# Token normalisation by bn_stats and ScalarE, and a projection moved behind the transposes, in a MetaFormer layer

## The chip, the cores and the metric

The kernel runs on one core of a Trainium2 chip. The metric is the device time of one execution in microseconds; before the change it is 7429.9 us, the median of 3 runs (7426.01 to 7444.18).

The names used here: TensorE (PE in the profile; PEld is its loading of weights) multiplies matrices, VectorE (DVE), ScalarE (ACT) and GpSimd (POOL) work on elements, SyncE (SP) issues transfers. SBUF is the memory beside the engines, PSUM the one that TensorE writes to. All of them run on their own and meet at semaphores.

## The reference, cut to what matters

```python
x = x + conv_ref(ln_c(x), wq, wk, wv, wo, rq, rk, rv, Gq, Gk, Gv1, Gv2)   # x: (4, 256, 128, 128) f32
t = to_tokens(x)                               # rows of 128 along w; 32768 tokens an image
t = t + ffn_ref(ln_t(t), gate_w, gate_b, weight1, weight2)

def ln_t(v, eps=1e-5):
    m = mean(v, axis=-1); s = var(v, axis=-1)
    return (v - m) / sqrt(s + eps)

# in ffn_ref: logits = x @ gate_w.T + gate_b (64 experts), softmax over the tokens,
# the 8 best tokens of each expert, the experts' two layers on them, added back to these tokens
```

Here conv_ref is an attention within each image row with relative terms, and ends in a 1x1 projection `wo`. The change lies between that projection and the logits: the sum with `x`, the normalisation ln_t of each row of 128, and the gate's logits. The reference is in float32 and so is all of the kernel.

## The kernel before, in words

The kernel is five phases that run one after the other: weights are prepared, q, k and v are projected, the attention is computed, `combine` finishes the attention and computes the gate's logits, and `experts` does the rest. The change touches `combine` alone.

`combine` works on 64 chunks, 16 for each of 4 images. A chunk is 8 image rows of all 256 channels: on the 128 partitions lie the channels of one half, so a chunk is two halves of 128 x 1024, or 16 groups (tokens) of 128 elements on each partition. Buffers come in pairs, used by even and odd chunks (`u`). For a chunk k the steps are:

- SyncE loads the two parts of the attention's sum (`sum_v`, `sum_r`) and x, 1 MB each in two transfers. The load of x waits for the residual of chunk k-2.
- GpSimd adds the two parts into `att` (line 888), after all six transfers have landed.
- TensorE projects (`project_out`, line 906): four blocks of 128 x 512, one for each PSUM bank of `y_ps`. Each block is two float32 matmuls, which the profile lists as four passes, so 16 passes a chunk. A block waits until VectorE has read the same bank of the chunk before.
- VectorE adds x to each block (`residual`, line 947); the result is `x1`.
- VectorE and ScalarE normalise with the class `LayerNorm`: VectorE sums each row (line 196), scales the 16 sums to means (line 198), subtracts them (line 203); ScalarE squares (line 207); VectorE sums the squares (line 212) and makes the variance (line 214); ScalarE takes the root (line 218); VectorE inverts it and refines the inverse in four short operations (lines 224 to 230) and multiplies (line 232) into `tn`.
- ScalarE issues the two stores of `x1` to the output (line 998), between the root and its next work.
- TensorE turns `tn` in 16 transposes (line 921) in four groups of four; ScalarE copies each group out of PSUM into `tnt` (line 1004). There are two banks for the turned groups, so a group waits for the copy of the group two before it.
- TensorE multiplies `tnt` by the gate (line 927) into `l_ps`, and ScalarE adds the bias and keeps the logits (`keep`, line 989).

The order on each engine is written out by hand, in a function `body(k, u, place)`, where `place` is 0 for an image's first chunk, 1 for the second, 14 and 15 for the last two, and 2 for the rest:

- TensorE's body: the projection of chunk k+2 (but at places 14 and 15), then the wait for `tn` of chunk k, its transposes, its logits. At place 0 it first projects k and k+1.
- VectorE's body: sums, means and centring of chunk k; the residual of chunk k+1; variance; inverse; the wait for the transposes that last read the buffer; the multiplication.
- ScalarE's body: the square of chunk k, `keep` of chunk k-1, the root of k, the stores of k, the four copies of k.

At the end of an image VectorE searches the logits for each expert's 8 largest, and ScalarE takes their exponentials, before the next image's chunks.

Of the kernel before, what the change touches and what calls it, by code (L numbers as in the profile page):

```python
# [17 lines left out]
P = 128  # L18
ALU = mybir.AluOpType
# [152 lines left out]
ROWS = 8  # L172
# [632 lines left out]
def combine(nc, d):  # L805

    with ExitStack() as ctx:
# [19 lines left out]
        y_ps = s.ps("y_ps", [P, 4, BANK])  # L828
        t_ps = s.ps("t_ps", [P, 2, BANK])
        l_ps = s.ps("l_ps", [P, 2, BANK])  # L830
        ln = LayerNorm(s, TOKEN_EPS)
        consts_loaded, ident_zero, ident_ready, gate_turned, gate_ready = (s.sem(n) for n in ("consts_loaded", "ident_zero", "ident_ready", "gate_turned", "gate_ready"))
        loaded = [s.sem(f"loaded{u}") for u in range(2)]
        att_ready, y_done, x1_ready, centred, tn_ready = (s.sem(n) for n in ("att_ready", "y_done", "x1_ready", "centred", "tn_ready"))
        turned, tnt_ready, l_done, l_ready = (s.sem(n) for n in ("turned", "tnt_ready", "l_done", "l_ready"))
        x1_stored = [s.sem(f"x1_stored{u}") for u in range(2)]
        cleared, topped, found, negated, summed, cand_stored = (s.sem(n) for n in ("cleared", "topped", "found", "negated", "summed", "cand_stored"))
# [55 lines left out]
        def _(pe):  # L893
# [3 lines left out]
            pe.transpose(t_ps[:, 0, 0:EXPERTS], gate[:, :], ident[0:EXPERTS, 0:EXPERTS]).then_inc(gate_turned, 1)  # L897
            pe.wait_ge(gate_ready, 1)

            def project_out(k, u):  # L900
                pe.wait_ge(att_ready, 2 * k + 6)
                for b in range(4):
                    sub, o = b // 2, b % 2
                    pe.wait_ge(x1_ready, 4 * k + b + 5)
                    for a in range(CHALF):
                        last = pe.matmul(y_ps[:, b], wo[:, a, o * P:(o + 1) * P], att[u][:, a, sub * BANK:(sub + 1) * BANK],  # L906
                                         start=a == 0, stop=a == CHALF - 1)
                    last.then_inc(y_done, 1)

            def body(k, u, place):  # L910
                if place == 0:
                    project_out(k, 0)
                    project_out(k + 1, 1)
                if place < PER - 2:
                    project_out(k + 2, u)
                pe.wait_ge(tn_ready, k + 1)
                for q in range(4):
                    pe.wait_ge(tnt_ready, 4 * k + q + 1)
                    a, rows = q // 2, range(4 * (q % 2), 4 * (q % 2) + 4)
                    for r, i in enumerate(rows):  # L920
                        last = pe.transpose(t_ps[:, q % 2, r * P:(r + 1) * P], tn[u][:, a * ROWS + i, :], ident[:, :])
                    last.then_inc(turned, 1)
                pe.wait_ge(tnt_ready, 4 * k + 6)
                for sub in range(2):
                    pe.wait_ge(l_ready, 2 * k + sub + 1)
                    for a in range(CHALF):
                        last = pe.matmul(l_ps[a * EXPERTS:(a + 1) * EXPERTS, sub], gate_t[:, :], tnt[:, 2 * a + sub, :], start=True, stop=True,
                                         tile_position=(0, a * EXPERTS))
                    last.then_inc(l_done, 1)
# [3 lines left out]
        @block.vector  # L933
        def _(dve):
            dve.sem_inc(x1_ready, 8)
            dve.wait_ge(gate_turned, 1)
            dve.tensor_copy(gate_t[:, :], t_ps[:, 0, 0:EXPERTS]).then_inc(gate_ready, 1)

            def residual(k, u, half_k):
                for b in range(4):  # L940
                    sub, o = b // 2, b % 2
                    dve.wait_ge(y_done, 4 * k + b + 9)
                    if b == 0:
                        dve.wait_ge(loaded[u], 8 * DMAS * k - 8 * DMAS * u + 16 * DMAS)
                        dve.wait_ge(x1_stored[u], 16 * k - 16 * u + 32)
                    at = slice(sub * BANK, (sub + 1) * BANK)
                    dve.tensor_tensor(x1[u][:, o, at], y_ps[:, b], x[u][:, o, at], ALU.add).then_inc(x1_ready, 1)  # L947

            def body(k, u, place):
                if place == 0:  # L950
                    residual(k, 0, 0)
                dve.wait_ge(x1_ready, 4 * k + 12)
                rows = x1[u][:, :, :].rearrange("c a (i w) -> c (a i) w", w=W)
                ln.mean_of(dve, rows, k)
                ln.centre(dve, rows, k).then_inc(centred, 1)
                if place < PER - 1:
                    residual(k + 1, 1 - u, 0)
                ln.variance(dve, k)
                dve.wait_ge(turned, 4 * k + 4)
                ln.scale(dve, tn[u][:, :, :], k).then_inc(tn_ready, 1)  # L960

            def best(n):
                dve.wait_ge(l_ready, 2 * PER * n + 2 * PER + 2)
# [12 lines left out]
        def _(act):  # L976
            act.sem_inc(turned, 8)
            act.sem_inc(tnt_ready, 2)
            act.sem_inc(l_ready, 2)
            act.sem_inc(cand_stored, 48)  # L980
            for u in range(2):
# [8 lines left out]
                                   ACT.Identity, bias=gate_b[:, :]).then_inc(l_ready, 1)  # L990

            def body(k, u, place):
                ln.square(act, centred, k + 1)
                if place:
                    keep(k - 1)
                ln.root(act, k)
                for a in range(CHALF):
                    act.dma_start(x1_out[bass.ds(k // PER, 1), :, a, bass.ds((k % PER) * CHUNK, CHUNK)].rearrange("n c x -> (n c) x"),
                                  x1[u][:, a, :]).then_inc(x1_stored[u], 16)
                for q in range(4):  # L1000
                    act.wait_ge(turned, 4 * k + q + 9)
                    if q == 0:
# [353 lines left out]
```

## Time and profile before

| | |
|---|---|
| median of 3 runs | 7429.9 us (7426.01 to 7444.18) |
| profiled execution, its own time | 7456.45 us |
| span of the profiled execution | 7454.4 us |
| granted TensorE clock, mean | 0.906 |
| busy: TensorE, its weight loads | 6396.6 us (86%), 5001.9 us (67%) |
| busy: VectorE, ScalarE, GpSimd | 5357.6 us (72%), 4765.6 us (64%), 2480.9 us (33%) |
| `combine`, by its first and last instructions | about 5854 to 7035 us of the span |

How to read it: a page and the answers of a query show one execution. Times are microseconds unless marked ns. A line such as `L232 DVE TENSOR_TENSOR comb_tn<-comb_ln_xc,...` names the source line, the engine, the operation and the tiles written and read. "x64" is a count.
### The profile page before, as it was taken

The numbers are of one execution on the slowest core, as the hardware profiler recorded it, in microseconds if no ns is written. First come the engines' busy times: TensorE is split into PE (matmuls) and PEld (weight loads), VectorE is DVE, ScalarE is ACT, GpSimd is POOL, SyncE is SP. The second block draws the span as 40 slices with busy tenths as digits, with TensorE's granted clock in tenths as the row PEclk, the third lists the DMA queues.
The fourth block names the chain that finished last, engine by engine and source line by source line (L and its number), as shares of the span: only waits on it lengthen the run. The fifth ranks groups of instructions, "written<-read, shape, count | busy, mean of one in ns | idle before, by whom it ended". The sixth has DMA issues, their size and how long they took to land. (4 is left out here: it accounts for less than half of the span.)

```text
span 7454.4 us, 279833 instructions
## 1 busy us (share of the span) xinstructions
PE 6396.6 (86%) x106442; PEld 5001.9 (67%) x106442; DVE 5357.6 (72%) x20905; ACT 4765.6 (64%) x11171; POOL 2480.9 (33%) x1267
## 2 busy tenths in 40 slices
PE   4999999969999989999998999989999767576558
PEld 3555555568888878888887888878888423232258
DVE  5444444448888878888887888878788788898820
ACT  0444444448988888888898898889889334343300
POOL 0000000025455545545554454544454323232110
PEclk6999999969999999999999999999999888898855
DMA  8555555557777677767677777777776767586422
GB/s 218 203 203 203 203 203 203 193 90 124 126 132 125 120 128 133 126 118 136 122 127 132 119 127 133 127 123 125 125 129 115 218 214 242 188 268 195 143 97 96
DMA packets 1197408, 1146.42 MB, mean 154 GB/s; under 512 B 625632, under 2 KB 956000, under 8 KB 1194144
## 3 DMA queue, kind: packets, MB, share of 16 engines
q1 hardware_dynamic: 1006816, 842.59, 54.6%
q10 hardware_dynamic: 188352, 285.27, 10.5%
q8 instruction: 795, 13.03, 0.9%
q14 instruction: 421, 3.45, 0.2%
q0 software_dynamic: 1024, 2.09, 0.1%
HBM read 708.04 MB, written 421.56 MB: 152 GB/s over the span
## 5 line engine op out<-in xcount | busy, mean ns | idle before, releaser
L788 POOL TENSOR_TENSOR att_scores<-att_scores,att_inverse 128x1024 f32<-128x1024 f32 x1024 | 1994.1, 1950 | 2047.0 <-DVE att_inverse L736 2046.8
L697 ACT ACTIVATE att_scores<-att_scores,att_negmax 128x128 f32<-128x128 f32 x8192 | 2572.9, 394 | 27.9 <-issue 13.2
L751 DVE CUSTOM_DVE_ANT_0 att_scores<-att_ps,att_scores 128x128 f32<-128x128 f32 x8192 | 1818.2, 289 | 773.1 <-PE att_ps L614 748.4
L603 PE MATMUL att_ps<-att_qk,att_rs 32*128 32x64 f32 x32768 | 2189.2, 280 | 107.1 <-issue 56.9
L603 PEld LDWEIGHTS att_ps<-att_qk,att_rs 32*128 32x128 f32 x32768 | 2034.2, 196 | 117.0 <-issue 110.0
L614 PE MATMUL att_ps<-att_own 32*128 32x128 f32 x16384 | 1822.0, 323 | 226.7 <-DMA att_own<-qk 150.0
L614 PEld LDWEIGHTS att_ps<-att_own 32*128 32x128 f32 x16384 | 1601.9, 198 | 512.5 <-issue 493.1
L656 PE MATMUL att_ps<-att_scores,att_rv 128*16 128x64 f32 x32768 | 1402.3, 330 | 39.0 <-issue 33.0
L690 ACT ACTIVATE att_scores<-att_ps 128x1024 f32<-128x1024 f32 x1024 | 1041.3, 1017 | 558.3 <-PE att_ps L603 528.7
L734 DVE TENSOR_REDUCE att_total<-att_scores 128x8 f32<-128x1024 f32 x1024 | 1242.2, 1213 | 0.0
L656 PEld LDWEIGHTS att_ps<-att_scores,att_rv 128*16 128x16 f32 x32768 | 1134.5, 119 | 71.6 <-issue 61.7
L369 PE MATMUL proj_qk_ps<-proj_xn,proj_w_qk 128*128 128x512 f32 x2048 | 902.8, 594 | 33.1 <-DVE proj_xn L232 33.1
L337 ACT ACTIVATE proj_qk_out<-proj_qk_ps 128x512 f32<-128x512 f32 x512 | 323.7, 632 | 613.5 <-PE proj_qk_ps L369 605.5
L369 PEld LDWEIGHTS proj_qk_ps<-proj_xn,proj_w_qk 128*128 128x128 f32 x2048 | 390.1, 191 | 470.5 <-issue 463.9
L906 PE MATMUL comb_y_ps<-comb_att,comb_wo 128*128 128x512 f32 x1024 | 514.3, 660 | 219.4 <-DVE comb_x L947 193.6
L751 DVE DVE_READ_ACCUMULATOR2_ANT att_negmax<- 128x1 f32 x8192 | 691.5, 84 | 0.3
L644 PE MATMUL att_ps<-att_scores,att_vt 128*16 128x128 f32 x16384 | 674.9, 282 | 17.0 <-issue 9.1
L784 POOL TENSOR_TENSOR att_rs<-att_rs,att_gain 128x1024 f32<-128x1024 f32 x64 | 122.4, 1913 | 1650.7 <-DMA att_rs<-in_L_conv_rk_dram 1650.7
L888 POOL TENSOR_TENSOR comb_att<-comb_sum_v,comb_sum_r 128x1024 f32<-128x1024 f32 x128 | 328.7, 2587 | 822.3 <-DMA comb_x<-in_x_dram 704.2
L906 PEld LDWEIGHTS comb_y_ps<-comb_att,comb_wo 128*128 128x128 f32 x1024 | 211.3, 212 | 527.3 <-issue 274.7
L377 PE MATMUL proj_v_ps<-proj_w_v,proj_xn 128*128 128x256 f32 x2048 | 462.9, 379 | 0.0
L377 PEld LDWEIGHTS proj_v_ps<-proj_w_v,proj_xn 128*128 128x128 f32 x2048 | 389.1, 190 | 107.5 <-issue 61.2
(147 smaller groups left out, 4986.3 us busy)
## 6 DMA issues: line engine op xcount, KB each, us to landing
qk<-proj_qk_out ACTq DMA_DIRECT2D x64, 2048.0 KB, 8.6
att_qk<-qk SPq DMA_DIRECT2D x512, 256.0 KB, 6.0
att_own<-qk SPq DMA_DIRECT2D x1024, 128.0 KB, 4.5
proj_x<-in_x_dram SPq DMA_DIRECT2D x128, 512.0 KB, 4.4
v_t<-proj_v_out ACTq DMA_DIRECT2D x64, 1024.0 KB, 11.7
att_vt<-v_t SPq DMA_DIRECT2D x256, 256.0 KB, 5.3
att_v<-att_att_v SPq DMA_DIRECT2D x1024, 64.0 KB, 3.8
att_r<-att_att_r SPq DMA_DIRECT2D x1024, 64.0 KB, 2.7
```

Of the source, the lines that this page charges most:

```text
L369: last = pe.matmul(qk_ps[:, j], w_qk[:, a, 4 * j:4 * j + 4].rearrange("c h t e -> c (h t e)"), xn[u][:, a, sub * BANK:(sub + 1) * BANK], s ...
L377: last = pe.matmul(v_ps[:, b, r * C:(r + 1) * C], xn[u][:, a, row * W:(row + 1) * W], w_v[:, a, :], start=a == 0, stop=a == CHALF - 1)
L603: return pe.matmul(ps[:, 4 + gg, jj * IU:(jj + 1) * IU], rs[32 * g:32 * g + 32, j, :], qk[v % 2][32 * g:32 * g + 32, :, j, :], start=True, ...
L614: return pe.matmul(ps[:, g, r * W:(r + 1) * W], own[half][32 * g:32 * g + 32, 1, at // PAIR, :, at % PAIR], own[half][32 * g:32 * g + 32, ...
L644: last = pe.matmul(ps[32 * g:32 * g + HD, 6, r * W:(r + 1) * W], vt[i // HROWS][:, i % HROWS, :], scores[v % BUFS][:, i, :], start=True, s ...
L656: last = pe.matmul(ps[32 * g:32 * g + HD, 7, jj * IU:(jj + 1) * IU], rv[:, j, :], scores[v % BUFS][:, :, j], start=True, stop=True, tile_p ...
L690: act.activation(scores[o % BUFS][:, :, :].rearrange("w i (g j) -> w i g j", g=G)[:, :, pair:pair + 2, t // 2 * JB:(t // 2 + 1) * JB], ps[ ...
L697: last = act.activation(scores[v % BUFS][:, i, :], scores[v % BUFS][:, i, :], ACT.Exp, bias=negmax[v % BUFS][:, i:i + 1], scale=-1.0)
L734: dve.tensor_reduce(piece(total[v], k), piece(scores[v], k), AX_X, ALU.add).then_inc(summed, 1)
L751: last = dve.tensor_tensor_reduce(out=scores[v][:, i, :], in0=ps[:, 2 * (p % 2) + r // HR, (r % HR) * W:(r % HR + 1) * W], in1=scores[v][: ...
L788: pool.tensor_tensor(piece(scores[v], p), piece(scores[v], p), piece(inverse[v], p).unsqueeze(3).broadcast_to([P, 2, HR, W]), ALU.mult).th ...
L906: last = pe.matmul(y_ps[:, b], wo[:, a, o * P:(o + 1) * P], att[u][:, a, sub * BANK:(sub + 1) * BANK], start=a == 0, stop=a == CHALF - 1)
```

## The change

The normalisation in `combine` no longer uses the class `LayerNorm`. VectorE takes mean and variance of two rows at a time with `bn_stats`, eight times for a chunk; the two rows are interleaved by the access pattern, as even and odd elements, so that one instruction gives both rows' count, mean and sum of squared deviations. One short operation makes the variance plus epsilon. After ScalarE's root, VectorE inverts and refines as before, and one more short operation makes `shift`, minus the mean times the inverse. ScalarE then normalises straight from `x1`: 16 activations of 128 x 128, each with its group's inverse as scale and its shift as bias.

The order changes with it. ScalarE's body is `keep` of k-1, root of k, stores of k, the 16 normalisations of k, the four copies of k. VectorE's body is the statistics of k, the residual of k+1, and inverse and shift of k; the residual now also waits until ScalarE has normalised the chunk that held the `x1` buffer before. TensorE's body is the wait for the normalised chunk, the first two groups of transposes, blocks 0 and 1 of the projection of k+2, the last two groups, blocks 2 and 3 of that projection, and the logits.

```diff
--- before.py
+++ after.py
@@ -828,10 +828,13 @@
         y_ps = s.ps("y_ps", [P, 4, BANK])
         t_ps = s.ps("t_ps", [P, 2, BANK])
         l_ps = s.ps("l_ps", [P, 2, BANK])
-        ln = LayerNorm(s, TOKEN_EPS)
+        stats = s.sb("stats", [P, GROUPS // 2, 2, 3])
+        var, std, inv, square, shift = (s.sb(n, [P, GROUPS]) for n in ("var", "std", "inv", "square", "shift"))
         consts_loaded, ident_zero, ident_ready, gate_turned, gate_ready = (s.sem(n) for n in ("consts_loaded", "ident_zero", "ident_ready", "gate_turned", "gate_ready"))
         loaded = [s.sem(f"loaded{u}") for u in range(2)]
-        att_ready, y_done, x1_ready, centred, tn_ready = (s.sem(n) for n in ("att_ready", "y_done", "x1_ready", "centred", "tn_ready"))
+        att_ready, y_done, x1_ready, tn_ready = (s.sem(n) for n in ("att_ready", "y_done", "x1_ready", "tn_ready"))
+        measured, var_ready, rooted, inverted, squared, corrected, refined, shifted = (
+            s.sem(n) for n in ("measured", "var_ready", "rooted", "inverted", "squared", "corrected", "refined", "shifted"))
         turned, tnt_ready, l_done, l_ready = (s.sem(n) for n in ("turned", "tnt_ready", "l_done", "l_ready"))
         x1_stored = [s.sem(f"x1_stored{u}") for u in range(2)]
         cleared, topped, found, negated, summed, cand_stored = (s.sem(n) for n in ("cleared", "topped", "found", "negated", "summed", "cand_stored"))
@@ -897,9 +900,10 @@
             pe.transpose(t_ps[:, 0, 0:EXPERTS], gate[:, :], ident[0:EXPERTS, 0:EXPERTS]).then_inc(gate_turned, 1)
             pe.wait_ge(gate_ready, 1)
 
-            def project_out(k, u):
-                pe.wait_ge(att_ready, 2 * k + 6)
-                for b in range(4):
+            def project_out(k, u, blocks=range(4)):
+                if 0 in blocks:
+                    pe.wait_ge(att_ready, 2 * k + 6)
+                for b in blocks:
                     sub, o = b // 2, b % 2
                     pe.wait_ge(x1_ready, 4 * k + b + 5)
                     for a in range(CHALF):
@@ -911,15 +915,15 @@
                 if place == 0:
                     project_out(k, 0)
                     project_out(k + 1, 1)
-                if place < PER - 2:
-                    project_out(k + 2, u)
-                pe.wait_ge(tn_ready, k + 1)
+                pe.wait_ge(tn_ready, k + 3)
                 for q in range(4):
                     pe.wait_ge(tnt_ready, 4 * k + q + 1)
                     a, rows = q // 2, range(4 * (q % 2), 4 * (q % 2) + 4)
                     for r, i in enumerate(rows):
                         last = pe.transpose(t_ps[:, q % 2, r * P:(r + 1) * P], tn[u][:, a * ROWS + i, :], ident[:, :])
                     last.then_inc(turned, 1)
+                    if q % 2 and place < PER - 2:
+                        project_out(k + 2, u, (q - 1, q))
                 pe.wait_ge(tnt_ready, 4 * k + 6)
                 for sub in range(2):
                     pe.wait_ge(l_ready, 2 * k + sub + 1)
@@ -933,6 +937,7 @@
         @block.vector
         def _(dve):
             dve.sem_inc(x1_ready, 8)
+            dve.sem_inc(shifted, 1)
             dve.wait_ge(gate_turned, 1)
             dve.tensor_copy(gate_t[:, :], t_ps[:, 0, 0:EXPERTS]).then_inc(gate_ready, 1)
 
@@ -943,21 +948,35 @@
                     if b == 0:
                         dve.wait_ge(loaded[u], 8 * DMAS * k - 8 * DMAS * u + 16 * DMAS)
                         dve.wait_ge(x1_stored[u], 16 * k - 16 * u + 32)
+                        dve.wait_ge(tn_ready, k + 1)
                     at = slice(sub * BANK, (sub + 1) * BANK)
                     dve.tensor_tensor(x1[u][:, o, at], y_ps[:, b], x[u][:, o, at], ALU.add).then_inc(x1_ready, 1)
 
             def body(k, u, place):
                 if place == 0:
                     residual(k, 0, 0)
+                dve.wait_ge(shifted, k + 1)
                 dve.wait_ge(x1_ready, 4 * k + 12)
-                rows = x1[u][:, :, :].rearrange("c a (i w) -> c (a i) w", w=W)
-                ln.mean_of(dve, rows, k)
-                ln.centre(dve, rows, k).then_inc(centred, 1)
+                rows = x1[u][:, :, :].rearrange("c a (b r w) -> c (a b) w r", r=2, w=W)
+                for g in range(GROUPS // 2):
+                    last = dve.bn_stats(stats[:, g].rearrange("c r m -> c (r m)"), rows[:, g])
+                last.then_inc(measured, 1)
+                dve.wait_ge(measured, k + 1)
+                dve.tensor_scalar(var[:, :].rearrange("c (g r) -> c g r", r=2), stats[:, :, :, 2], 1.0 / W, TOKEN_EPS, ALU.mult, ALU.add).then_inc(var_ready, 1)
                 if place < PER - 1:
                     residual(k + 1, 1 - u, 0)
-                ln.variance(dve, k)
-                dve.wait_ge(turned, 4 * k + 4)
-                ln.scale(dve, tn[u][:, :, :], k).then_inc(tn_ready, 1)
+                dve.wait_ge(rooted, k + 1)
+                dve.wait_ge(tn_ready, k + 2)
+                dve.reciprocal(inv[:, :], std[:, :]).then_inc(inverted, 1)
+                dve.wait_ge(inverted, k + 1)
+                dve.tensor_tensor(square[:, :], inv[:, :], inv[:, :], ALU.mult).then_inc(squared, 1)
+                dve.wait_ge(squared, k + 1)
+                dve.scalar_tensor_tensor(out=square[:, :], in0=square[:, :], scalar=-0.5, in1=var[:, :], op0=ALU.mult, op1=ALU.mult).then_inc(corrected, 1)
+                dve.wait_ge(corrected, k + 1)
+                dve.scalar_tensor_tensor(out=inv[:, :], in0=square[:, :], scalar=1.5, in1=inv[:, :], op0=ALU.add, op1=ALU.mult).then_inc(refined, 1)
+                dve.wait_ge(refined, k + 1)
+                dve.scalar_tensor_tensor(out=shift[:, :].rearrange("c (g r) -> c g r", r=2), in0=stats[:, :, :, 1], scalar=-1.0,
+                                         in1=inv[:, :].rearrange("c (g r) -> c g r", r=2), op0=ALU.mult, op1=ALU.mult).then_inc(shifted, 1)
 
             def best(n):
                 dve.wait_ge(l_ready, 2 * PER * n + 2 * PER + 2)
@@ -976,6 +995,7 @@
         def _(act):
             act.sem_inc(turned, 8)
             act.sem_inc(tnt_ready, 2)
+            act.sem_inc(tn_ready, 2)
             act.sem_inc(l_ready, 2)
             act.sem_inc(cand_stored, 48)
             for u in range(2):
@@ -990,13 +1010,19 @@
                                    ACT.Identity, bias=gate_b[:, :]).then_inc(l_ready, 1)
 
             def body(k, u, place):
-                ln.square(act, centred, k + 1)
                 if place:
                     keep(k - 1)
-                ln.root(act, k)
+                act.wait_ge(var_ready, k + 1)
+                act.activation(std[:, :], var[:, :], ACT.Sqrt).then_inc(rooted, 1)
                 for a in range(CHALF):
                     act.dma_start(x1_out[bass.ds(k // PER, 1), :, a, bass.ds((k % PER) * CHUNK, CHUNK)].rearrange("n c x -> (n c) x"),
                                   x1[u][:, a, :]).then_inc(x1_stored[u], 16)
+                act.wait_ge(shifted, k + 2)
+                act.wait_ge(turned, 4 * k + 4)
+                for r in range(GROUPS):
+                    last = act.activation(tn[u][:, r, :], x1[u][:, r // ROWS, (r % ROWS) * W:(r % ROWS + 1) * W], ACT.Identity,
+                                          bias=shift[:, r:r + 1], scale=inv[:, r:r + 1])
+                last.then_inc(tn_ready, 1)
                 for q in range(4):
                     act.wait_ge(turned, 4 * k + q + 9)
                     if q == 0:
```

## Rows read from the trace of the kernel before

**Rows 1.** The page: span, and busy time of each engine with its share.

```profile
span 7454.4 us, 279833 instructions
...
PE 6396.6 (86%) x106442; PEld 5001.9 (67%) x106442; DVE 5357.6 (72%) x20905; ACT 4765.6 (64%) x11171; POOL 2480.9 (33%) x1267
```

**Rows 2.** Groups by line, 5840 to 7050 us: busy, mean ns | idle before.

```profile
...
L232 DVE TENSOR_TENSOR comb_tn<-comb_ln_xc,comb_ln_inv 128x2048 f32<-128x2048 f32 x64 | 146.7, 2292 | 2.2
...
L989 ACT ACTIVATE comb_logits<-comb_l_ps,comb_gate_b 128x512 f32 (+1 forms) x128 | 131.5, 1121 | 11.4 <-PE comb_l_ps L927 11.3
L198 DVE TENSOR_SCALAR comb_ln_mean<-comb_ln_t 128x16 f32<-128x16 f32 x64 | 127.0, 1985 | 2.2
```

**Rows 3.** Window: busy PE, PEld, DVE, ACT, POOL; PEclk; DMA share; GB/s.

```profile
...
5870.00:6100.00 230.00, 169.37 (x564) 77.19 (x562) 215.29 (x208) 90.80 (x115) 79.11 (x31) 0.93 0.81 269
```

**Rows 4.** Line 232 in each image: duration min/median/max in ns, first and last start.

```profile
L232 DVE TENSOR_TENSOR comb_tn<-comb_ln_xc,comb_ln_inv x16: 2291/2292/2293, 5876.5 to 6113.1; 128x2048 f32<-128x2048 f32 x16
...
L232 DVE TENSOR_TENSOR comb_tn<-comb_ln_xc,comb_ln_inv x16: 2291/2292/2294, 6183.1 to 6419.3; 128x2048 f32<-128x2048 f32 x16
...
L232 DVE TENSOR_TENSOR comb_tn<-comb_ln_xc,comb_ln_inv x16: 2291/2292/2293, 6490.2 to 6722.6; 128x2048 f32<-128x2048 f32 x16
...
L232 DVE TENSOR_TENSOR comb_tn<-comb_ln_xc,comb_ln_inv x16: 2291/2292/2293, 6793.2 to 7020.7; 128x2048 f32<-128x2048 f32 x16
```

**Rows 5.** Timeline of all engines, 5999.5 to 6012.7 us: start, duration, engine, line.

```profile
...
5999.92 0.82 SPq L875 DMA_DIRECT2D comb_x<-in_x_dram  x2
...
6002.32 0.22 ACT L218 ACTIVATE comb_ln_std<-comb_ln_var 128x16 f32<-128x16 f32 x1 [1.72 <-DVE comb_ln_var L214]
...
6002.63 0.85 ACTq L998 DMA_DIRECT2D out_dram<-comb_x  x2
...
6003.56 2.29 DVE L232 TENSOR_TENSOR comb_tn<-comb_ln_xc,comb_ln_inv 128x2048 f32<-128x2048 f32 x1
...
6004.99 5.39 POOL L888 TENSOR_TENSOR comb_att<-comb_sum_v,comb_sum_r 128x1024 f32<-128x1024 f32 x2 [10.62 <-DMA comb_x<-in_x_dram]
...
6005.98 1.09 PE L921 MATMUL comb_t_ps<-comb_ident,comb_tn 128*128 128x128 f32 x8 [0.70 <-DVE comb_tn L232]
6006.75 1.09 ACT L1004 ACTIVATE comb_tnt<-comb_t_ps 128x512 f32<-128x512 f32 x2 [4.21 <-PE comb_t_ps L921]
...
6008.08 2.33 DVE L198 TENSOR_SCALAR comb_ln_mean<-comb_ln_t 128x16 f32<-128x16 f32 x1
```

**Rows 6.** Timeline of TensorE alone, 5850 to 6420 us, idle before in brackets.

```profile
...
5875.37 9.96 PE L906 MATMUL comb_y_ps<-comb_att,comb_wo 128*128 128x512 f32 x16 [3.77 <-POOL comb_att L888]
...
6160.39 9.11 PE L906 MATMUL comb_y_ps<-comb_att,comb_wo 128*128 128x512 f32 x16 [29.61 <-DVE comb_x L947]
...
6185.55 3.85 PE L921 MATMUL comb_t_ps<-comb_ident,comb_tn 128*128 128x128 f32 x16 [6.50 <-DVE comb_tn L232]
6190.17 3.68 PE L927 MATMUL comb_l_ps<-comb_tnt,comb_gate_t 128*64 128x512 f32 x8 [0.76 <-ACT comb_tnt L1004]
...
6201.39 1.04 PE L921 MATMUL comb_t_ps<-comb_ident,comb_tn 128*128 128x128 f32 x8
6202.76 1.15 PE L921 MATMUL comb_t_ps<-comb_ident,comb_tn 128*128 128x128 f32 x8 [0.33 <-ACT comb_tnt L1004]
6204.67 1.94 PE L927 MATMUL comb_l_ps<-comb_tnt,comb_gate_t 128*64 128x512 f32 x8 [0.76 <-ACT comb_tnt L1004]
6207.32 7.13 PE L906 MATMUL comb_y_ps<-comb_att,comb_wo 128*128 128x512 f32 x16 [0.71 <-DVE comb_x L947]
...
6406.78 3.68 PE L921 MATMUL comb_t_ps<-comb_ident,comb_tn 128*128 128x128 f32 x16 [10.07 <-DVE comb_tn L232]
6411.22 1.94 PE L927 MATMUL comb_l_ps<-comb_tnt,comb_gate_t 128*64 128x512 f32 x8 [0.76 <-ACT comb_tnt L1004]
```

**Rows 7.** Line 697's exponentials on ScalarE: duration min/median/max in ns.

```profile
...
L697 ACT ACTIVATE att_scores<-att_scores,att_negmax x8192: 376/388/458, 1579.4 to 5807.1; 128x128 f32<-128x128 f32 x200
```

**Rows 8.** Timeline of ScalarE in the attention stage, 3002 to 3006 us.

```profile
...
3002.62 2.48 ACT L697 ACTIVATE att_scores<-att_scores,att_negmax 128x128 f32<-128x128 f32 x8
```

## The prediction, made before the changed kernel was run

> **What bounds the kernel now.** I read the page's first part, then the combine stage alone (the change touches nothing else): its groups by line, its busy time by window, and one chunk as a timeline. The profiled execution takes 7456.45 us, its span 7454.4 us [rows 1]. In 230 us of steady combine work VectorE is busy 215.3 us, TensorE 169.4 us, ScalarE 90.8 us, at a granted TensorE clock of 0.93 and a DMA share of 0.81 [rows 3]. VectorE is the bound: a chunk puts four passes over 2048 elements on it (the last, line 232, takes 2.29 us [rows 2]) and a negligible-looking scaling of 16 means that takes 1.99 us on average [rows 2], because it is held: in the timeline it starts at 6008.08 while GpSimd runs since 6004.99, and ends at 6010.41, when GpSimd ends at 6010.38 [rows 5]. The period of a chunk comes from line 232: per image 16 executions, first to last start 236.6, 236.2, 232.4 and 227.5 us [rows 4], together 932.7 us for 60 periods, 15.55 us each. TensorE's projection hides in it, issued ahead of the wait for the normalised chunk, while VectorE and ScalarE still work on that chunk.
>
> **The order after the change.** I followed the semaphores round one chunk before pricing anything. ScalarE's body for chunk k starts with keep(k-1), which waits for the logits of k-1. Only then, in order, come the root for k, the two stores' issue, the wait for the shifts, 16 normalisations, the signal that the chunk is ready. TensorE's body for k now starts with the wait for that signal; the projection stands behind it, and the logits of k stand behind both halves of the projection. And keep(k), with which ScalarE's next body starts, needs these logits. So the two engines take turns: TensorE's whole body, then ScalarE's keep, root and normalisations, then TensorE again. Nothing of one body overlaps the other but four copies out of PSUM. Before, the projection (7.13 us [rows 6]) ran beside VectorE's work; now it is in the ring. The period is the sum of the ring.
>
> **Term by term.**
> - VectorE loses its four long passes and the held scaling and gains 8 bn_stats, of 256 elements each. No row shows one; the 2.29 us for 2048 elements gives 0.29 us each in proportion, 2.3 us in all; the ends are 0.17 us each (below the 128x16 operations' own time nothing runs here) and 2.29 us each. They run for chunk k+1 while ScalarE normalises k and TensorE works on k: cover of more than 15 us, so I count nothing at either end but the very last (18 us), which would be late by a few us. VectorE stops being the bound; what is late next is the ring.
> - Hand-over from normalised chunk to TensorE: 0.13 us (line 232 ends at 5.85, the transpose starts at 5.98 [rows 5]).
> - TensorE at the full clock: 8 transposes 1.04, half a projection 3.56, 8 transposes 1.15, half a projection 3.56, logits 1.94 [rows 6]: 11.25 us. The copies between them (1.09 us for two [rows 5]) lie beside the first half and the second. I keep 11.2.
> - TensorE's clock: after the ring's ScalarE part TensorE has been idle for some 9 us. Rows show what an idle stretch does: after 3.77 and 29.6 us idle a projection of 16 passes takes 9.96 and 9.11 us instead of 7.13, mean 2.4 us more; after 6.5 us idle transposes and logits take 3.85 and 3.68 us, logits at half their pace, yet after 10.07 us idle the clock is back for the logits, 1.94 us [rows 6]. So each body starts at 1.2 GHz and recovers inside it. Ends: nothing (the clock stays up), and half pace throughout, 1.9 + 1.9 for transposes, 14.3 for the projection, 3.68 for the logits, 10.6 us more than 11.2. I take 2.9: the 2.4 of a projection plus half of the 0.9 that cold first transposes cost (3.85/2 against 1.04).
> - Logits to root: two keeps of 1.12 us [rows 2], the first begun when half of the logits is there: 1.15 us past the end of the logits.
> - Root to shifts: from the root's start (6002.32) to line 232's (6003.56) 1.24 us [rows 5], plus one more operation like those between, 0.2, and a hand-over: 1.48 us. The stores' issue (0.85 us on ScalarE's queue [rows 5]) lies beside it.
> - 16 normalisations of 128x128. The nearest row is the exponential of line 697: 388 ns each alone [rows 7], 8 back to back in 2.48 us [rows 8], 0.30 us from start to start. Ends: 15 x 0.30 + 0.39 = 4.9 us with full overlap, 16 x 0.458 (its longest [rows 7]) = 7.3 us. I take 16 x 0.388 = 6.2 us, without overlap, because each reads two operands per partition (bias and scale) where the exponential reads one.
>
> The Trainium skill (ScalarE: Activation LUTs, What ACT_TABLE_LOAD costs) says that an operand given per partition adds about 93 ns to an ACTIVATE and that neighbours overlap by about 93 ns. The 388 ns and the 0.30 us from start to start agree with it for one such operand; no row has two. By that page 16 would take about 6.3 us, an estimate; by the row's own overlap 4.9.
>
> Ring: 0.13 + 11.2 + 2.9 + 1.15 + 1.48 + 6.2 = 23.06 us, against 15.55. Memory does not bind it: 0.81 x 15.55 = 12.6 us of transfer a chunk [rows 3]. GpSimd's addition runs two chunks ahead.
>
> In an image 14 periods hold a projection; the 15th does not: transposes and logits with their gap, 6.4 to 8.3 us by the rows after idling [rows 6], say 7.4, and 0.13 + 1.15 + 1.48 + 6.2: 16.4 us. So 14 x 23.06 + 16.4 = 339.2 us an image, 1357 us for four, against 932.7: +424 us. The head of an image loses a square and a reduction and gains the 16 normalisations; I count nothing, within 1 us an image. The candidates' search is untouched. Profiled execution 7456.45 + 424 = 7880; it lies 26.5 us above the median of the runs (7429.9), so the forecast is 7854 us.
>
> **The rivals.**
> - The clock is not lost, because projection, transposes and logits now stand close together: the ring is 20.2 us, 56 x 2.9 = 162 us less, 7692 us; with the overlapped normalisations too 7619. For it: the one body after 10 us of idling that recovered in its transposes. Against: every body now follows a long idle stretch.
> - The clock never recovers: 10.6 instead of 2.9, 56 x 7.7 = 431 us more, 8285 us. For it: the transposes and logits that ran at half pace through all 8.3 us [rows 6]. Against: both projections after idling ended less than 3 us late.
> - GpSimd holds the short VectorE operations of root to shifts, as it holds the scaling of the means: 2.33 - 0.17 = 2.16 us a chunk, 60 x 2.16 = 130 us, 7984 us. It decides when GpSimd starts inside these 1.3 us. GpSimd starts 5.07 us after the load of x is issued (5999.92 to 6004.99 [rows 5]), and that load now follows the last residual, about 0.8 us after the projection; root to shifts runs 3.3 to 4.6 us after the projection. By that it is 1.3 us clear. The Trainium skill (SBUF — State Buffer, Who interferes with whom) calls this an exclusive lock and extends it to VectorE operations with two SBUF inputs, which three of these are; the held scaling agrees, and no row here shows it for two inputs.
> - Other side, faster: TensorE and ScalarE do overlap, and the relief of VectorE shows. The place is keep(k-1) at the head of ScalarE's body: if the part beside TensorE's 11.2 us fitted into 4.3 us the period would pass below 15.55. Keep, root and hand-over take 2.8 of these, so the 16 normalisations would have to take 1.5 us, under 0.1 us each, a third of the tightest spacing that a row shows. Then the transfers' 12.6 us would bound: 60 x 2.95 = 177 us less, 7253 us.
> - The change doesn't do what it says: VectorE's relief and the ring cancel. That takes a ring of 15.5 us, and the same 0.1 us each.
>
> **How the numbers follow.** Forecast 70%, own range 7700 to 8000 (normalisations 4.9 to 7.3 us, clock 1.7 to 4.2: 20.5 to 25.5 us of ring, 56 of each). Clock kept 10%, clock never back 7%, GpSimd in the way 8%, faster 3%, cancelled 2%. From 7690 to 8010 the forecast, most of the GpSimd case and part of the clock case are inside. A change of 0.3% (22 us) is what a measurement can tell; slower 95%, same 2%, faster 3%.
>
> **What would show it.** In the changed kernel TensorE idle for 8 to 10 us between logits and first transpose, its releaser the normalisations; ScalarE waiting for the logits before keep; the first transposes and part of the first half of the projection at 1.2 GHz, the second half at 2.4; normalisations from start to start near 0.39 us; VectorE under half busy, its small operations between root and shift 0.2 us each. Wrong it is if keep(k-1) starts before the second half of the projection has ended, or if the period stays under 18.8 us (the ring at the full clock with overlapped normalisations).

## The result, and the profile after

The changed kernel takes 7794.72 us (median of 4 runs, 7783.66 to 7805.79) against 7427.95 us before (median of 4 runs; the 7429.9 us of the first table are the median of three of them): 1.0492 times as long, 95% interval 1.0475 to 1.0509, 367 us more. The forecast was 7854 us, slower, with a range from 7690 to 8010. The profiled execution of the changed kernel lies 11 us above its median, the one before 28.5 us, so the two profiles differ by less than the medians: 7803.8 against 7454.4 us of span [rows 1], 349 us.

The page, and 220 us of the first image by window (columns as in [rows 3]):

```profile
span 7803.8 us, 280727 instructions
...
PE 6427.9 (82%) x106442; PEld 5044.1 (65%) x106442; DVE 4916.4 (63%) x21161; ACT 5042.9 (65%) x12131; POOL 2456.5 (31%) x1267
```

```profile
5890.00:6110.00 220.00, 128.58 (x400) 64.45 (x400) 75.44 (x181) 107.26 (x236) 48.74 (x22) 0.78 0.59 194
```

VectorE lost 441 us of work over the kernel and is busy for 34% of the stage instead of 94%. No engine is busy for more than 59% of it. The relief is real and the stage is longer: engines wait for each other. How long a chunk takes, by the shift (line 978), which every chunk makes once; first and last start of each image, as in [rows 4]:

```profile
L978 DVE SCALAR_TENSOR_TENSOR comb_shift<-comb_stats,comb_inv x16: 174/175/176, 5863.0 to 6184.3; 128x16 f32<-128x16 f32 x16
...
L978 DVE SCALAR_TENSOR_TENSOR comb_shift<-comb_stats,comb_inv x16: 174/174/176, 6257.6 to 6577.4; 128x16 f32<-128x16 f32 x16
...
L978 DVE SCALAR_TENSOR_TENSOR comb_shift<-comb_stats,comb_inv x16: 174/174/176, 6650.9 to 6972.1; 128x16 f32<-128x16 f32 x16
...
L978 DVE SCALAR_TENSOR_TENSOR comb_shift<-comb_stats,comb_inv x16: 174/175/176, 7045.1 to 7365.8; 128x16 f32<-128x16 f32 x16
```

Together 1283.0 us for 60 periods, 21.4 us each, against 932.7 us and 15.55 before: 350 us more, which is all of the difference between the two profiles. One period on the timeline of all engines:

```profile
6033.00 1.94 PE L931 MATMUL comb_l_ps<-comb_tnt,comb_gate_t 128*64 128x512 f32 x8
...
6034.27 2.00 ACT L1009 ACTIVATE comb_logits<-comb_l_ps,comb_gate_b 128x512 f32 x2 [3.95 <-PE comb_l_ps L931]
...
6036.07 0.22 ACT L1016 ACTIVATE comb_std<-comb_var 128x16 f32<-128x16 f32 x1
...
6037.24 0.18 DVE L978 SCALAR_TENSOR_TENSOR comb_shift<-comb_stats,comb_inv 128x16 f32<-128x16 f32 x1
6037.45 2.74 DVE L962 BATCH_NORM_STATS2 comb_stats<-comb_x 128x6 f32<-128x256 f32 x8
6037.54 6.26 ACT L1023 ACTIVATE comb_tn<-comb_x,comb_shift,comb_inv 128x128 f32<-128x128 f32 x16 [1.25 <-DVE comb_shift L978]
...
6040.26 4.65 POOL L891 TENSOR_TENSOR comb_att<-comb_sum_v,comb_sum_r 128x1024 f32<-128x1024 f32 x2 [16.46 <-DMA comb_x<-in_x_dram]
6043.93 1.96 PE L923 MATMUL comb_t_ps<-comb_ident,comb_tn 128*128 128x128 f32 x8 [8.99 <-ACT comb_tn L1023]
...
6045.68 5.54 PE L910 MATMUL comb_y_ps<-comb_att,comb_wo 128*128 128x512 f32 x8
...
6051.06 1.04 PE L923 MATMUL comb_t_ps<-comb_ident,comb_tn 128*128 128x128 f32 x8
...
6051.94 3.60 PE L910 MATMUL comb_y_ps<-comb_att,comb_wo 128*128 128x512 f32 x8
...
6055.47 1.94 PE L931 MATMUL comb_l_ps<-comb_tnt,comb_gate_t 128*64 128x512 f32 x8
```

Read it as two turns. ScalarE sits idle for 3.95 us until the logits come, then keeps them, takes the root, and normalises until 6043.80. TensorE sits idle for 8.99 us all that while, and starts 0.13 us later. Its first 8 transposes take 1.75 us from start to start and the last 8 take 0.88; the first half of the projection 5.38 and the second 3.53: the first of each pair ran wholly or in part at the lower clock. The granted clock is 0.50 in the first transposes, 0.63 in the first half and 1.00 in the second half.

### The profile page after: what moved, and what is told of

Its sections match the earlier page's. It is cut to its first block and busy times, and to the rows that moved or that the text cites. A ratio compares the mean times of both kernels' runs of the same rounds, so it can differ in the third digit from the quotient of the medians.

```text
span 7803.8 us, 280727 instructions
## 1 busy us (share of the span) xinstructions
PE 6427.9 (82%) x106442; PEld 5044.1 (65%) x106442; DVE 4916.4 (63%) x21161; ACT 5042.9 (65%) x12131; POOL 2456.5 (31%) x1267
## 5 line engine op out<-in xcount | busy, mean ns | idle before, releaser
L923 PE MATMUL comb_t_ps<-comb_ident,comb_tn 128*128 128x128 f32 x1024 | 198.0, 358 | 604.8 <-ACT comb_tn L1023 604.8
L644 PE MATMUL att_ps<-att_scores,att_vt 128*16 128x128 f32 x16384 | 675.1, 282 | 18.6 <-issue 12.2
L891 POOL TENSOR_TENSOR comb_att<-comb_sum_v,comb_sum_r 128x1024 f32<-128x1024 f32 x128 | 297.5, 2346 | 1193.1 <-DMA comb_x<-in_x_dram 1189.1
L910 PE MATMUL comb_y_ps<-comb_att,comb_wo 128*128 128x512 f32 x1024 | 543.2, 682 | 103.7 <-DVE comb_x L953 87.9
L923 PEld LDWEIGHTS comb_t_ps<-comb_ident,comb_tn 128*128 128x128 f32 x1024 | 164.5, 186 | 693.9 <-issue 690.9
L953 DVE TENSOR_TENSOR comb_x<-comb_y_ps,comb_x 128x512 f32<-128x512 f32 x256 | 176.0, 691 | 670.0 <-PE comb_y_ps L910 435.1
```

The source lines that it names most:

```text
L644: last = pe.matmul(ps[32 * g:32 * g + HD, 6, r * W:(r + 1) * W], vt[i // HROWS][:, i % HROWS, :], scores[v % BUFS][:, i, :], start=True, s ...
```

## The experiments

Theory: a ring. The projection stands in it, between the normalised chunk and the logits, and ScalarE's turn follows the logits. Rivals: ScalarE's normalisations are dear wherever the projection stands; the lost clock makes up most of it.

The kernel before was run again beside each group of runs. Its medians were 7427.95 us beside the changed kernel, 7447.2 beside e1 to e4, 7430.4 beside e5 to e8 and 7437.7 beside e9. Each ratio is to its own one of these; a difference between kernels of two groups can be off by some 20 us.

**The projection alone moved back (e1_ahead).** bn_stats and ScalarE's normalisations stay.

```diff
+                if place < PER - 2:
+                    project_out(k + 2, u)
                 pe.wait_ge(tn_ready, k + 3)
...
-                    if q % 2 and place < PER - 2:
-                        project_out(k + 2, u, (q - 1, q))
```

> The changed kernel with the projection of k+2 whole again and ahead of the wait for the normalised chunk; bn_stats and ScalarE's normalisations stay. Theory of the ring (TensorE's body and ScalarE's keep, root and normalisations take turns, and the projection's place puts it into the ring): the projection runs beside ScalarE's turn; ring 0.13 + transposes, copies and logits 5.2 + 1.15 + 1.5 + 6.3 = 14.3 us a chunk against 21.9, with a little of the clock lost 14.3 to 15.3; time 7330 to 7430 us, not slower than the kernel before. Rival (the normalisations on ScalarE are the cost, wherever the projection stands): above 7650 us.

Measured: 7650.6 us, 1.026 times before (1.022 to 1.030). The theory's range was missed, and the median lies on the very bound of the rival's: 144 us of the change's 367 came back, not all. So the time alone does not decide. The timeline shows two things that the sum had left out:

```profile
6014.45 4.66 POOL L891 TENSOR_TENSOR comb_att<-comb_sum_v,comb_sum_r 128x1024 f32<-128x1024 f32 x2 [14.56 <-DMA comb_x<-in_x_dram]
...
6016.79 2.35 DVE L972 TENSOR_TENSOR comb_square<-comb_inv 128x16 f32<-128x16 f32 x1
...
6019.89 6.26 ACT L1023 ACTIVATE comb_tn<-comb_x,comb_shift,comb_inv 128x128 f32<-128x128 f32 x16 [3.42 <-DVE comb_shift L978]
...
6026.28 3.85 PE L925 MATMUL comb_t_ps<-comb_ident,comb_tn 128*128 128x128 f32 x16 [3.96 <-ACT comb_tn L1023]
...
6030.89 3.68 PE L931 MATMUL comb_l_ps<-comb_tnt,comb_gate_t 128*64 128x512 f32 x8 [0.76 <-ACT comb_tnt L1030]
```

The earlier residual makes x land earlier, GpSimd's addition starts beside the short operations, and one of them waits until GpSimd ends (6016.79 + 2.35 = 6019.14; GpSimd 6014.45 + 4.66 = 6019.11). ScalarE's wait for the shift grows from 1.25 to 3.42 us; TensorE idles for 3.96 us, and its transposes and logits run at the lower clock (3.85 us for 16 and 3.68 us). This is the prediction's GpSimd rival, in another kernel.

**The same, with GpSimd out of the way (e8_ahead_unlocked).** GpSimd's body for chunk k also waits until the shift of k-3 is made (the semaphore starts two higher, so that the value stays positive).

```diff
                     pool.wait_ge(y_done, 4 * k + 4)
+                    pool.wait_ge(shifted, k + 1)
```

> The kernel with the projection ahead of the wait (keep at the head of the body), and GpSimd's addition for chunk k+3 waits for the shift of k, so that it never runs beside the short operations between root and shift. In the kernel without this wait two of these took 1.38 and 1.32 us on average instead of 0.17 and 0.21. Theory that GpSimd holds VectorE's operations with two SBUF inputs: they fall back to 0.17 us each, 64 x 2.3 = 150 us less than the 7651 us, 7480 to 7530 us. Rival (the durations came from something else, or the later addition only moves the wait): above 7620 us.

Measured: 7448.1 us, 1.0026 times before (1.0006 to 1.0045), 202 us less than without the wait and 32 us under what the theory gave. Groups of the stage (busy, mean ns | idle before), and a stretch of the timeline:

```profile
L966 DVE TENSOR_SCALAR comb_var<-comb_stats 128x16 f32<-128x16 f32 x64 | 87.1, 1361 | 2.2
...
L975 DVE SCALAR_TENSOR_TENSOR comb_square<-comb_square,comb_var 128x16 f32<-128x16 f32 x64 | 13.3, 208 | 2.2
L973 DVE TENSOR_TENSOR comb_square<-comb_inv 128x16 f32<-128x16 f32 x64 | 11.2, 175 | 2.2
```

```profile
6021.28 4.67 POOL L892 TENSOR_TENSOR comb_att<-comb_sum_v,comb_sum_r 128x1024 f32<-128x1024 f32 x2 [10.35 <-DMA comb_x<-in_x_dram]
...
6026.96 1.09 PE L926 MATMUL comb_t_ps<-comb_ident,comb_tn 128*128 128x128 f32 x8 [1.94 <-ACT comb_tn L1024]
```

The two operations are back at 0.18 and 0.21 us (1.38 and 1.32 without the wait: 150 us over 64 chunks). GpSimd now holds the variance instead (1.36 us), of which the ring takes no notice. The other 50 us go with the clock: TensorE idles 1.94 us instead of 3.96 here, and its first transposes run at 1.09 us for 8. From first transpose to last logit all 64 chunks take 436.8 us against 482.9 in e1_ahead, 46 us less. The clock is not back throughout. All periods but the first are of two kinds: 14.1 to 14.3 us, which is the ring's sum at the full clock, where this turn of TensorE takes 5.27 us, and 16.4 to 17.1 us, where the logits run at half pace and the turn takes 7.5 to 8.3. So the normalisation's part of the change, with the projection left ahead of the wait, is worth nothing by itself even with GpSimd out of the way: it costs 0.3%.

**The projection's move alone, in the kernel before (e2_move_only).**

```diff
-                if place < PER - 2:
-                    project_out(k + 2, u)
                 pe.wait_ge(tn_ready, k + 1)
...
+                    if q % 2 and place < PER - 2:
+                        project_out(k + 2, u, (q - 1, q))
```

> The kernel before with the one edit that the projection stands in two halves behind the second and fourth transposed block; the normalisation is the old one. Theory of the ring: VectorE's residual of k+2 now waits for a projection that itself waits for the normalised k, and variance, root and the multiplication stand behind that residual: 0.1 + 9.4 + 0.75 + 2.5 + 1.2 + 2.3 = 16.3 us and 1 to 2.3 of clock, 17.3 to 18.6 us against 15.55; 7530 to 7620 us. Rival (the place of the projection is harmless, the long ScalarE part does the harm): within 30 us of 7428.

Measured: 7531.9 us, 1.011 times before (1.0075 to 1.015), 85 us more, at the lower edge of what the ring gave; a chunk takes 16.9 us against 15.5, a little under the 17.3 to 18.6 of that sum. VectorE works through part of TensorE's turn there (in its timeline the sums, means and centring take 7.0 us from 6024.57 on, the transposes start at 6024.78), so the same move costs less than in the changed kernel (7794.7 against e8_ahead_unlocked's 7448.1, with GpSimd's hold out of the way in both: some 345 us).

**TensorE's idle stretch filled (e3_filled).**

```diff
                     last.then_inc(l_done, 1)
+                for j in range(9):
+                    pe.matmul(t_ps[:, j % 2], wo[:, 0, 0:P], wo[:, :, :].rearrange("c a o -> c (a o)"), start=True, stop=True)
```

> The changed kernel with 9 extra matmuls of 128x512 behind each chunk's logits, into the PSUM banks of the transposed blocks, whose result nothing reads: they fill about 7.7 of the 9 us in which TensorE is idle at the full clock. Theory that the clock lost to the idle stretch costs 0.9 us in the first transposes and 1.4 in the first half of the projection of each chunk: the first 8 transposes fall from 1.96 to 1.1 us, the first half to 3.6, the granted clock of the stage rises from 0.78 to near 1, 2.3 x 60 = 130 to 140 us less than the changed kernel, 7650 to 7690 us. Rival (these durations are not the idle stretch's doing, or extra matmuls delay the next chunk): 7790 or more.

Measured: 7687.1 us, 108 us less than the changed kernel, within what the theory gave. The window of the changed kernel above, here, and a row of its timeline:

```profile
5890.00:6110.00 220.00, 208.09 (x653) 94.82 (x652) 87.31 (x200) 116.48 (x255) 51.24 (x22) 1.00 0.65 210
```

```profile
6023.56 1.09 PE L923 MATMUL comb_t_ps<-comb_ident,comb_tn 128*128 128x128 f32 x8 [1.08 <-ACT comb_tn L1025]
```

The granted clock is 1.00 instead of 0.78, the 8 transposes take 1.09 instead of 1.96 us. The clock is a share of the loss, some 30%; the greater part of it is the turns.

**One operand less in the normalisations (e4_one_operand).** The output lacks the shift. The function changes too, from Identity to Copy.

```diff
-                    last = act.activation(tn[u][:, r, :], x1[...], ACT.Identity,
-                                          bias=shift[:, r:r + 1], scale=inv[:, r:r + 1])
+                    last = act.activation(tn[u][:, r, :], x1[...], ACT.Copy, scale=inv[:, r:r + 1])
```

> The changed kernel with normalisations that multiply only and leave the shift out, so each reads one operand per partition instead of two; everything else stays, the shift is still computed and waited for. Theory that the second operand costs about 0.09 us of each normalisation: 0.478 falls to 0.39 us, 16 from 6.26 to 4.8 us, 64 x 1.45 = 93 us less than the changed kernel, about 7700 us. Rival (the duration does not hang on the operands): 0.478 stays, 7795 us.

Measured: 7720.5 us, 74 us less, where the theory gave 93. Duration of one in ns (min/median/max), and 16 of them on the timeline:

```profile
L1023 ACT ACTIVATE comb_tn<-comb_x,comb_inv x1024: 384/386/402, 5858.4 to 7283.0; 128x128 f32<-128x128 f32 x171
```

```profile
6020.64 4.79 ACT L1023 ACTIVATE comb_tn<-comb_x,comb_inv 128x128 f32<-128x128 f32 x16 [1.25 <-DVE comb_shift L978]
```

386 ns against 478, 4.79 us against 6.26 for 16: with one operand less each takes 0.092 us less. That the function makes it is unlikely, since the exponential, another function with one operand, takes 388 ns [rows 7]. Most of it stands in the ring: of the 1.47 us, a chunk whose period holds a projection gives back 1.39 by the starts of line 978 (20.40 against 21.79 us), the last period of an image nothing (15.7 in both).

**Keep behind the normalisations (e5_keep_late), and with the projection ahead too (e6_both).**

```diff
             def body(k, u, place):
-                if place:
-                    keep(k - 1)
                 act.wait_ge(var_ready, k + 1)
...
                 last.then_inc(tn_ready, 1)
+                if place:
+                    keep(k - 1)
                 for q in range(4):
```

> The changed kernel with one edit on ScalarE: keep of k-1 stands behind the 16 normalisations of k instead of at the head of the body. Theory of the ring: logits and keep leave it, but the inverse of k+1 still stands behind the residual of k+2, which waits for the second half of the projection behind the transposes of k: 0.13 + 4.0 + 5.0 + 0.9 + 3.6 less what overlaps, in all 19 to 20 us against 21.9, 7660 to 7700 us. Rival (keep at the head of the body was the whole link between the engines): the ring falls to 15 us and the time below 7450.

> Both orders changed: the projection whole and ahead of the wait, and keep of k-1 behind the normalisations of k. Theory of the ring: it shrinks to ScalarE's own work, keep 2.0, four copies with their waits 3, root 0.2, wait for the inverse 1.25, normalisations 6.3 = 12.8 us, near the 12.6 us that the transfers take; GpSimd's addition would start 1 to 2 us behind the short VectorE operations; 13 to 14.5 us a chunk, 7270 to 7370 us, faster than the kernel before. Rival (GpSimd holds the short operations here as it did in the kernel with the projection ahead, 2.4 us a chunk): 7420 to 7500 us.

Measured: 7644.6 us (1.0275 times before, 1.024 to 1.031), a little under what the ring gave, and 7252.8 us (0.976, 0.972 to 0.979), 17 us under it, faster than both kernels. With keep moved alone the ring stays closed by another way, as forecast. In e5_keep_late, on the timeline, the root is ready long before the inverse begins, because VectorE has the residual of the next chunk in between, and that waits for the projection:

```profile
6033.64 0.22 ACT L1014 ACTIVATE comb_std<-comb_var 128x16 f32<-128x16 f32 x1
...
6036.54 0.69 DVE L953 TENSOR_TENSOR comb_x<-comb_y_ps,comb_x 128x512 f32<-128x512 f32 x1 [1.03 <-PE comb_y_ps L910]
...
6037.15 0.24 DVE L970 RECIPROCAL comb_inv<-comb_std 128x16 f32<-128x16 f32 x1
```

With both moves the ring is ScalarE's own work, with a wait of 1.25 us in it. Its timeline in e6_both, a period of 12.1 us, the projection (7.13 us) beside the normalisations:

```profile
5992.26 6.26 ACT L1021 ACTIVATE comb_tn<-comb_x,comb_shift,comb_inv 128x128 f32<-128x128 f32 x16 [1.25 <-DVE comb_shift L978]
5992.90 7.13 PE L910 MATMUL comb_y_ps<-comb_att,comb_wo 128*128 128x512 f32 x16
...
5998.43 2.03 ACT L1009 ACTIVATE comb_logits<-comb_l_ps,comb_gate_b 128x512 f32 x2
...
6002.92 0.21 ACT L1014 ACTIVATE comb_std<-comb_var 128x16 f32<-128x16 f32 x1
...
6004.37 6.26 ACT L1021 ACTIVATE comb_tn<-comb_x,comb_shift,comb_inv 128x128 f32<-128x128 f32 x16 [1.24 <-DVE comb_shift L978]
```

**The root earlier (e7_early_root), and GpSimd's wait on top (e9_early_unlocked).** On top of both moves the root of k+1 stands right behind the normalisations of k, ahead of keep; in the second GpSimd waits for the shift as above.

```diff
                 last.then_inc(tn_ready, 1)
+                if place < PER - 1:
+                    root(k + 1)
                 if place:
                     keep(k - 1)
```

> As the kernel with both orders changed, and the root of k+1 stands right behind the normalisations of k, ahead of keep, so that VectorE's inverse of k+1 is made while ScalarE keeps logits and copies. Theory of the ring: ScalarE's wait for the inverse goes, 1.4 us a chunk less where ScalarE binds, down to the transfers' 12.6 us; 7250 to 7330 us, 20 to 80 below the kernel with both orders. Rival (the transfers bind already): the same as with both orders, within 15 us.

> The kernel with both orders changed and the early root, and GpSimd's addition for k+3 waits for the shift of k. The early root was worth 10 us only, against 20 to 80 expected. Theory that GpSimd's hold took the rest back (in that kernel the first two operations with two SBUF inputs took 0.60 and 0.34 us on average instead of 0.26 and 0.21): they fall to 0.17 us and up to 64 x 0.5 = 30 us go, 7210 to 7230 us. Rival (the held operations stand beside ScalarE's copies, so they cost nothing; the copies and the loads set the period): within 12 us of 7243.

Measured: 7242.8 us (0.974 times before, 0.971 to 0.977) and 7270.4 us (0.978, 0.977 to 0.980). The early root is within 15 us of e6_both, as its rival (the transfers bind already) had it; the intervals overlap, so no gain is shown. The transfers' share speaks for that rival. The same 120 us of steady work, columns as in [rows 3], in e6_both and in e7_early_root:

```profile
5900.00:6020.00 120.00, 106.20 (x392) 50.39 (x390) 67.68 (x180) 103.80 (x229) 46.81 (x20) 1.00 1.04 347
```

```profile
5900.00:6020.00 120.00, 109.22 (x393) 51.65 (x394) 63.50 (x174) 104.12 (x229) 46.78 (x20) 1.00 1.03 343
```

The DMA share, a mean over 16 engines that can pass 1 in this view, is 1.04 and 1.03, where the kernel before has 0.80 in this window. No run took a transfer away, so this is argued, not shown.

Whether GpSimd's hold took the early root's gain back, e9_early_unlocked does not settle, because its wait hardly lifted the hold. Two groups of it:

```profile
L973 DVE TENSOR_TENSOR comb_square<-comb_inv 128x16 f32<-128x16 f32 x64 | 35.1, 549 | 2.2
L975 DVE SCALAR_TENSOR_TENSOR comb_square<-comb_square,comb_var 128x16 f32<-128x16 f32 x64 | 17.5, 273 | 2.2
```

They take 0.55 and 0.27 us on average, against 0.60 and 0.34 without the wait. The time is 28 us higher, beyond what either theory gave (20 us when each is taken against its own runs of the kernel before), and the chunks are not where it goes: 60 periods take 721.0 us against 718.7. It goes between the images, where ScalarE is idle ahead of a table load for 14.6, 11.8 and 13.2 us, against 2.3 to 2.6 in e7_early_root, with nothing in the profile that it waits for. Why is open.

In e7_early_root the operations are still held now and then, but mostly beside ScalarE's copies: in its window from 5900 to 6060 us ScalarE never waits more than 1.2 us for the shift. Waits of that window (total, times, longest):

```profile
DVE comb_x L953 <- DMA out_dram<-comb_x: 31.0, 6, 6.7
...
ACT comb_tn L1025 <- DVE comb_shift L978: 8.8, 9, 1.2
```

The residual waits for the stores of the chunk that held its buffer, as it does in e6_both (29.4 us in 7 waits there). Whether the transfers or ScalarE's own work set the last 12 us of a chunk wasn't tried.

## Why the prediction was right, point by point

- **The order round a chunk.** Right: TensorE's idle stretch of 8.99 us ends with the normalisations, ScalarE's of 3.95 us with the logits, as forecast. e6_both shows that the ring opens when both edges are moved, and e5_keep_late that it stays closed when keep is moved alone.
- **TensorE at the full clock.** 11.2 forecast. From the period shown, 0.88 + 3.53 + 0.88 + 3.53 + 1.94 = 10.76 us, since the ends of the 8-pass groups overlap the next by up to 0.17 us; the sum had added their durations.
- **The clock.** 2.9 forecast, the largest miss. In e3_filled 60 periods take 1166.4 us instead of 1283.0: 1.9 us a chunk. The changed kernel's own trace agrees: from first transpose to last logit a chunk with a projection takes 12.82 us on average, 2.1 more than the 10.76. The sum charged a whole projection's recovery and half of the cold transposes; the first half of the projection lost between 0.5 and 2.2 us (4.09 to 5.77 us for it in the first image, against 3.60), less than the 2.4 of a projection with no transposes in front.
- **Logits to root** 1.13 in the period shown, 1.09 on average, for 1.15, **root to shifts** 1.47 for 1.48, **hand-over** 0.13.
- **The normalisations.** 6.26 us for 6.2, and that close by luck: not 16 of 0.388 without overlap, but 0.478 each, overlapped to 0.385 from start to start; two errors cancel. What the Trainium skill states (ScalarE: Activation LUTs, What ACT_TABLE_LOAD costs), 0.093 us for each operand per partition and as much of overlap, agrees with 0.478 against 0.386 us here, and the estimate of 6.3 worked out from it with 6.26.
- **The sum.** 14 x 23.06 + 16.4 = 339.2 us an image was forecast and 320.8 measured. In the second image the last period is 15.2 us and the other 14 take 21.8: 1.3 us less than forecast, by the two points above about 1.0 for the clock and 0.4 for the overlap in TensorE's body. Over four images that is 74 us; the profile of before lies higher above its median than that of after, which gives back 15, and 59 are left between 7854 and 7795.
- **VectorE's cover.** bn_stats takes 2.74 us for 8, and its variance was held by GpSimd (1.02 us on average, against 0.17 in the period shown); none of it reached the ring.
- **The rivals.** The clock neither stayed up nor stayed down. GpSimd's hold did not happen, but in the first chunk of each image: in the period shown its addition started 2.8 us behind the shift, not 1.3. That it is real shows in e1_ahead, also for an operation with two SBUF inputs (2.35 us against 0.17). The Trainium skill (SBUF — State Buffer, Who interferes with whom) states it for such operations, and the trace agrees. Four of the short operations have two such inputs, not three.
- **A number beside the sum:** the 12.6 us given as the transfers' bound. e6_both and e7_early_root take 12.1 and 12.0 us a chunk in mid-image, some 4% under it, so it is no exact floor. It is near one: the share passes 1 there, and 1.04 times 12.1 is 12.6 again. It decided nothing at 23 us.

## What to carry to other kernels

Taking work off the busiest engine is worth only what the order lets through: follow the semaphores round one iteration first, and see whether two engines take turns. A piece of work that stands ahead of a wait can be free there, and behind it it can stand in the ring: TensorE's turn at the full clock grew from 5.27 us (e8_ahead_unlocked) to 10.76, and the idle stretch cost clock on top. What it costs depends on what else works meanwhile: the same move was worth 1.4 us a chunk in the kernel before. When an order is changed, look again at what now starts beside what: in e1_ahead an earlier load brought GpSimd beside four operations of 0.2 us and cost 2.5 us a chunk.

## What the runs showed of the hardware that was not expected

bn_stats (BATCH_NORM_STATS2) over 256 interleaved float32 elements takes 0.416 us alone and 0.33 us from start to start (8 in 2.74). A GpSimd addition does not hold it: 284 of those in e8_ahead_unlocked ran wholly beside one and took 0.404 to 0.445 us. A normalisation on ScalarE takes 0.092 us more with its second operand per partition. VectorE's operations of 16 elements took 2.3 us beside a GpSimd addition, whether tensor_scalar with one SBUF input or tensor_tensor with two; the reciprocal right in front of them was never held (0.243 to 0.255 us in all 64 of e1_ahead, 40 of which ran wholly beside an addition).
